# Graph network of four layers: masks of the edge sums made for four tiles by one instruction, records waited for by fours

## The chip, the cores and the metric

One core of one Trainium2 chip. The metric is the device time of one execution in microseconds; before the change it is 5067.49 us, the median of three runs (5064.09 to 5072.64). Differences of about 0.2%, 10 us, can be told from none.

## The reference

6250 nodes with 256 features (x), 100000 edges sorted by target (src, dst), with 128 attributes, a type (0 to 15) and a weight. Each of four layers adds to x what it makes of h = relu(layernorm(x)):

```python
# layer 0: weighted sums by source
out = segment_sum((h @ weight)[dst] * edge_weight[:, None], src) + b
# layer 1: sums of edge attributes by source, degrees, two gates
h + z_in[in_deg] + z_out[out_deg] + cent_term + vor_term + segment_sum(edge_attr @ W_sum + b_sum, src)
# layer 2: attention over the edges of a target, then a feed-forward part
# layer 3: sums by target of neighbour rows and relation vectors, then a GRU cell
red = segment_sum(h[src] + relvectors[edge_type], dst)
out = gru_cell(red, h, w_ih, w_hh, b_ih, b_hh)
```

Everything is float32. Layers 0 and 1 need sums by source, layer 3 sums by target.

## The kernel before

All stages work on edges that are sorted and cut into 832 tiles of 128 edges (TILES); the nodes stand in 49 blocks of 128 (BLOCKS), and each tile holds edges of one block. A sum over the edges of a tile is a product on TensorE (PE): a mask (hot) with a one in row e, column n where edge e belongs to node n of the block, times the rows of the 128 edges. VectorE (DVE) makes the mask by comparing the row of numbers 0 to 127 (iota) with the edge's local node, and adds the product from PSUM to the block's sums in SBUF.

The stages follow each other:

1. `prepare`: ranks the edges by source and scatters their records (attributes, source, weight, target) to `src_records`, 784 indirect DMAs by POOL (L462).
2. `sources_and_layers_0_1`: per tile SP loads 128 records (L932), POOL gathers 128 rows of h (`gather`, L983), DVE makes `hot` (`hots`, L1198) and `hotw`, hot times the weight (`weigh`, L1203), PE makes two products (`sum_rows`, L1018, L1019), DVE adds them (`add`, L1211). Between the tiles the steps of layers 0 and 1 for each finished block are woven in, one block each 16 tiles: among them two gathers of z by POOL (`gather_z`, L993) that wait for degrees from DVE, and two powers by POOL (`root`, L1003) that wait for variances from DVE (L1282).
3. `attention`: 832 tiles with gathers (L1398), masks and products of its own.
4. `layer_2`, dense work on blocks.
5. `relations_and_layer_3`: per tile POOL gathers 128 rows (L2005), DVE makes `hot` (L2178) and, in columns 256 to 271 of the gathered row, the mask of the edge's type (L2182), PE makes one product (L2046), DVE adds it (L2190). The steps of the GRU are woven in.

The helper `woven` writes out each engine's order by hand: at position n it calls each step of a tile with a lag, step(n - lag), and each step of a block at its own position. In stage 2 DVE runs at position n: add of tile n-4 (LAG), weigh of n-1, hots of n, then node steps; all node steps of DVE stand DVE_LEAD = 2 positions behind the listed ones, those of POOL POOL_LEAD = 5 behind. Each engine runs its queue in order and waits at semaphores. Rings: 16 slots for records and rows (R), 8 for masks (H), 4 PSUM banks for the sums. A slot's reuse waits for PE's count of finished tiles (`summed`), a bank's reuse for DVE's count of adds. POOL waits for each tile's record with `own_wait`, a wait and a nop.

## Time and profile before

| | us |
|---|---|
| median of three runs | 5067.49 |
| lowest, highest | 5064.09, 5072.64 |
| span of the profiled execution | 6606.6 |
| PE busy in it | 3748.5 |
| DVE busy | 3700.6 |
| POOL busy | 3595.2 |
| ACT busy | 1475.8 |

Only the span is told of the profiled execution; it is 1539.1 us longer than the median of the runs without recording. The stages' borders in it are read from POOL's and the other engines' first and last instructions: prepare up to 1499 us, sums by source 1499 to 3152, attention to 4911, layer 2 to 5226, relations to the end. The chain of waits covers only the last per cent of the span, so it isn't used.

### The profile page before, as it was taken

The numbers are of one execution on the slowest core, as the hardware profiler recorded it, in microseconds if no ns is written. First come the engines' busy times: TensorE is split into PE (matmuls) and PEld (weight loads), VectorE is DVE, ScalarE is ACT, GpSimd is POOL, SyncE is SP. The second block draws the span as 40 slices with busy tenths as digits, with TensorE's granted clock in tenths as the row PEclk, the third lists the DMA queues.
The fourth block names the chain that finished last, engine by engine and source line by source line (L and its number), as shares of the span: only waits on it lengthen the run. The fifth ranks groups of instructions, "written<-read, shape, count | busy, mean of one in ns | idle before, by whom it ended". The sixth has DMA issues, their size and how long they took to land. (4 is left out here: it accounts for less than half of the span.)

```text
span 6606.6 us, 98591 instructions
## 1 busy us (share of the span) xinstructions
PE 3748.5 (57%) x15612; PEld 2748.4 (42%) x15613; DVE 3700.6 (56%) x12722; ACT 1475.8 (22%) x5078; POOL 3595.2 (54%) x4000
## 2 busy tenths in 40 slices
PE   0000020005776776776677777777779667777676
PEld 0000010004555554555455555555559534444443
DVE  5249691006666666666555555555557656555555
ACT  1000000000111111111455455555546301100000
POOL 4640686755655565555444444444437766655554
PEclk9999999998887888888788888878889878888888
DMA  4320224454444444444333333333332233333332
GB/s 119 85 68 0 73 83 89 118 148 120 127 127 123 125 128 124 127 128 111 93 94 94 96 95 95 94 93 94 97 95 86 89 88 94 91 91 90 90 90 72
DMA packets 505174, 651.54 MB, mean 99 GB/s; under 512 B 86113, under 2 KB 381294, under 8 KB 504944
## 3 DMA queue, kind: packets, MB, share of 16 engines
q0 software_dynamic: 150160, 395.04, 20.9%
q1 hardware_dynamic: 354913, 255.45, 14.3%
q14 instruction: 73, 0.60, 0.0%
q8 instruction: 28, 0.46, 0.0%
HBM read 550.09 MB, written 100.06 MB: 98 GB/s over the span
## 5 line engine op out<-in xcount | busy, mean ns | idle before, releaser
L1398 POOL DMA_INDIRECT a_row<-h_rows,a_idx x832 | 789.8, 949 | 944.0 <-PE a_p_s L1504 396.0
L2005 POOL DMA_INDIRECT r_row<-h_rows,r_idx x832 | 798.3, 960 | 528.7 <-PE r_p_s L2046 267.9
L462 POOL DMA_INDIRECT src_records<-rec,pos_slot x784 | 808.2, 1031 | 419.6 <-issue 250.3
L983 POOL DMA_INDIRECT s_row<-h_rows,s_rec x832 | 804.5, 967 | 281.0 <-issue 242.2
L1018 PE MATMUL s_sums<-s_row,s_hotw 128*128 128x256 f32 x1664 | 661.3, 484 | 519.5 <-DVE s_hotw L1203 315.3
L2046 PE MATMUL r_p_s<-r_row,r_hot 128*128 128x272 f32 x1664 | 644.8, 502 | 362.8 <-DVE r_row L2182 171.9
L1481 PE MATMUL a_p_q<-nodes,a_hotT 128*128 x1664 | 665.0, 486 | 314.9 <-DVE a_score L1551 188.9
L1211 DVE TENSOR_TENSOR nodes<-nodes,s_sums 128x385 f32 x832 | 455.5, 548 | 509.1 <-remote 290.8
L1504 PE MATMUL a_p_s<-a_row,a_masked 128*128 128x257 f32 x1664 | 588.7, 439 | 178.1 <-issue 124.3
L2046 PEld LDWEIGHTS r_p_s<-r_row,r_hot 128*128 128x128 f32 x1664 | 353.1, 234 | 678.8 <-issue 296.2
L1551 DVE CUSTOM_DVE_ANT_0 a_prod<-a_p_q,a_row 128x258 f32<-128x258 f32 x832 | 352.7, 424 | 415.9 <-DMA s_rec<-src_records 187.6
L1018 PEld LDWEIGHTS s_sums<-s_row,s_hotw 128*128 128x128 f32 x1664 | 301.9, 223 | 677.5 <-DVE s_hotw L1203 373.2
L1588 DVE SCALAR_TENSOR_TENSOR sums<-sums,a_fade,a_p_s 128x257 f32 x832 | 399.9, 481 | 263.1 <-DMA s_row<-h_rows,s_rec 141.5
L2190 DVE TENSOR_TENSOR sums<-sums,r_p_s 128x272 f32 x832 | 358.1, 430 | 300.5 <-PE r_p_s L2046 137.5
L1504 PEld LDWEIGHTS a_p_s<-a_row,a_masked 128*128 128x128 f32 x1664 | 353.1, 221 | 287.1 <-issue 183.7
L576 PE MATMUL p_total<-cnt,ones 128*128 128x49 f32 x4 | 1.3, 432 | 813.9 <-issue 783.3
L1481 PEld LDWEIGHTS a_p_q<-nodes,a_hotT 128*128 128x128 f32 x1664 | 293.7, 221 | 334.7 <-issue 333.2
L1019 PEld LDWEIGHTS s_sums<-s_rec,s_hot 128*128 128x128 f32 x1664 | 374.8, 225 | 69.4
L1433 ACT ACTIVATE a_masked<-a_far,a_score 128x128 f32<-128x128 f32 x832 | 326.5, 392 | 224.7 <-issue 191.8
L1019 PE MATMUL s_sums<-s_rec,s_hot 128*128 128x129 f32 x1664 | 368.4, 308 | 0.0
L576 PEld LDWEIGHTS p_total<-cnt,ones 128*128 128x128 f32 x4 | 1.0, 312 | 813.7 <-issue 783.5
L1496 PEld LDWEIGHTS a_p_l<-a_m,a_hotT 128*128 128x128 f32 x1664 | 291.2, 219 | 84.1 <-issue 33.8
(315 smaller groups left out, 7511.6 us busy)
## 6 DMA issues: line engine op xcount, KB each, us to landing
s_rec<-src_records SPq DMA_DIRECT2D x832, 66.0 KB
a_locs<-dloc_rows SPq DMA_DIRECT2D x208, 256.0 KB
rec<-in_edge_attr SPq DMA_DIRECT2D x98, 448.0 KB
s_row<-h_rows,s_rec POOLq DMA_INDIRECT x832
a_row<-h_rows,a_idx POOLq DMA_INDIRECT x832
r_row<-h_rows,r_idx POOLq DMA_INDIRECT x832
src_records<-rec,pos_slot POOLq DMA_INDIRECT x784
x_rows<-X SPq DMA_DIRECT2D x1, 6272.0 KB
```

The source lines that it names most:

```text
L462: gp.indirect_dma_start(out=src_records, out_offset=bass.IndirectOffsetOnAxis(ap=pos_slot[:, k:k + 1], axis=0), in_=rec[:, k, :], in_offse ...
L983: gp.indirect_dma_start(out=row[:, k % R, :], out_offset=None, in_=env["h0_rows"], in_offset=bass.IndirectOffsetOnAxis(ap=rec[:, k % R, DS ...
L1018: nc.tensor.matmul(bank[:, 0:D], hotw[:, k % H, :], row[:, k % R, :], start=True, stop=True)
L1019: nc.tensor.matmul(bank[:, D:NW], hot[:, k % H, :], rec[:, k % R, 0:ED + 1], start=True, stop=True).then_inc(summed, 1)
L1211: nc.vector.tensor_tensor(s, s, sums[k % BANKS][:, 0:NW], ALU.add).then_inc(block_added, 1)
L1398: gp.indirect_dma_start(out=row[:, k, 0:D], out_offset=None, in_=env["h2_rows"], in_offset=bass.IndirectOffsetOnAxis(ap=idx[:, k:k + 1], a ...
L1481: nc.tensor.matmul(p_q[k % 2], hotT[:, k % F, :], query[:, bass.ds(b, 1), 0:RW].rearrange("p a d -> p (a d)"), start=True, stop=True).then ...
L1504: nc.tensor.matmul(p_s[k % 2], masked[:, k % F, :], row[:, k, 0:D + 1], start=True, stop=True).then_inc(S["summed"], 1)
L1588: nc.vector.scalar_tensor_tensor(out=s, in0=s, scalar=fade[:, k % F:k % F + 1], in1=p_s[k % 2], op0=ALU.mult, op1=ALU.add).then_inc(S["add ...
L2005: gp.indirect_dma_start(out=row[:, k % R, 0:D], out_offset=None, in_=env["h3_rows"], in_offset=bass.IndirectOffsetOnAxis(ap=idx[:, k:k + 1 ...
L2046: nc.tensor.matmul(p_s[k % 4], hot[:, k % H, :], row[:, k % R, :], start=True, stop=True).then_inc(S["summed"], 1)
L2190: nc.vector.tensor_tensor(s, s, p_s[k % 4], ALU.add).then_inc(S["added"], 1)
```

## The change

In stage 2 the rings of masks grow to 16 slots. At every fourth tile DVE does for four tiles at once: `locate` (new; source minus the block's base, 4 columns), `hots` (iota equal to that column) and `weigh` (mask times weight), each one `tensor_tensor` with broadcast operands where there was one `tensor_scalar` per tile. The adds are done 8 tiles behind, and DVE's node steps stand 4 positions later. The four records of a group signal one semaphore; POOL waits once in four tiles, PE for the weighted masks too. In stage 5 the two masks are made for four tiles by one instruction each, the type masks first; the mask ring stays at 8 slots.

```diff
+FOUR = 4
@@ sources_and_layers_0_1
-    R, H = SLOT, UNROLL
-    LAG = 4
+    R, H = SLOT, SLOT
+    BLOCKS_READ = UNROLL
+    LAG = 8
-    SP_LEAD, POOL_LEAD, DVE_LEAD = 16, 5, 2
+    SP_LEAD, POOL_LEAD, DVE_LEAD = 16, 5, 6
+        local = sb(ctx, "s_local", [P, H])
-        rec_in = [sem(f"s_rec_in{k}") for k in range(R)]
+        rec_in = [sem(f"s_rec_in{k}") for k in range(R // FOUR)]
+        def four_of(k, g):
+            return g * (WOVEN // FOUR) + k // FOUR
+        def slot_in(eng, k, g):
+            eng.wait_ge(rec_in[k % R // FOUR], turn_of(k, g) * (16 * FOUR) + 16 * FOUR)
...
                 def gather(i, k, opening, g):
-                    own_wait(gp, rec_in[k % R], turn_of(k, g) * 16 + 16)
+                    if k % FOUR == 0:
+                        slot_in(gp, k, g)
+                        gp.nop(nofuse=True)
...
                 def sum_rows(i, k, opening, g):
-                    pe.wait_ge(hotw_ready, i + 1)
+                    if k % FOUR == 0:
+                        pe.wait_ge(hotw_ready, four_of(k, g) + 1)
...
+                def locate(i, k, opening, g):
+                    if k % FOUR:
+                        return
+                    slot_in(ve, k, g)
+                    if not opening or k >= H:
+                        ve.wait_ge(hot_ready, four_of(k, g) - (H // FOUR - 1))
+                    nc.vector.tensor_tensor(local[:, slots(k)].rearrange("p (k o) -> p k o", o=1), rec[:, slots(k), SRC:SRC + 1],
+                                            pbase[:, bass.ds(i, FOUR)].rearrange("p (k o) -> p k o", o=1), ALU.subtract
+                                            ).then_inc(local_ready, 1)
                 def hots(i, k, opening, g):
-                    ve.wait_ge(rec_in[k % R], turn_of(k, g) * 16 + 16)
+                    if k % FOUR:
+                        return
+                    ve.wait_ge(local_ready, four_of(k, g) + 1)
                     if not opening or k >= H:
-                        ve.wait_ge(summed, i - H + 1)
-                    nc.vector.tensor_scalar(hot[:, k % H, :], c["iota"][:], pbase[:, bass.ds(i, 1)], rec[:, k % R, SRC:SRC + 1],
-                                            ALU.add, ALU.is_equal).then_inc(hot_ready, 1)
+                        ve.wait_ge(summed, i - (H - FOUR))
+                    nc.vector.tensor_tensor(hot[:, slots(k), :], c["iota"].rearrange("p (a n) -> p a n", a=1).broadcast_to([P, FOUR, P]),
+                                            column(local[:, slots(k)].rearrange("p (k o) -> p k o", o=1)), ALU.is_equal
+                                            ).then_inc(hot_ready, 1)
                 def weigh(i, k, opening, g):
-                    ve.wait_ge(hot_ready, i + 1)
-                    nc.vector.tensor_scalar(hotw[:, k % H, :], hot[:, k % H, :], rec[:, k % R, WGT:WGT + 1], None,
+                    if k % FOUR:
+                        return
+                    ve.wait_ge(hot_ready, four_of(k, g) + 1)
+                    nc.vector.tensor_tensor(hotw[:, slots(k), :], hot[:, slots(k), :], column(rec[:, slots(k), WGT:WGT + 1]),
                                             ALU.mult).then_inc(hotw_ready, 1)
...
-                woven(ve, (LAG, add), (1, weigh), (0, hots), once={24: [key_bias]}, begin=load_blocks,
+                woven(ve, (LAG, add), (2, weigh), (1, hots), (0, locate), once={24: [key_bias]}, begin=load_blocks,
@@ relations_and_layer_3
                 def sum_rows(i, k, opening, g):
-                    pe.wait_ge(S["hot_ready"], i * 2 + 2)
+                    if k % FOUR == 0:
+                        pe.wait_ge(S["hot_ready"], (g * (WOVEN // FOUR) + k // FOUR) * 2 + 2)
...
                 def hots(i, k, opening, g):
+                    if k % FOUR:
+                        return
+                    if not opening or k >= R:
+                        ve.wait_ge(S["summed"], i - (R - FOUR))
+                    nc.vector.tensor_tensor(row[:, k % R:k % R + FOUR, D:DW], row_of(RELS), column(c["dtyp"], i, RELS),
+                                            ALU.is_equal).then_inc(S["hot_ready"], 1)
                     if not opening or k >= H:
-                        ve.wait_ge(S["summed"], i - H + 1)
-                    nc.vector.tensor_scalar(hot[:, k % H, :], c["iota"][:], c["dloc"][:, bass.ds(i, 1)], None,
-                                            ALU.is_equal).then_inc(S["hot_ready"], 1)
-                    if not opening or k >= R:
-                        ve.wait_ge(S["summed"], i - R + 1)
-                    nc.vector.tensor_scalar(row[:, k % R, D:DW], c["iota"][:, 0:RELS], c["dtyp"][:, bass.ds(i, 1)], None,
+                        ve.wait_ge(S["summed"], i - (H - FOUR))
+                    nc.vector.tensor_tensor(hot[:, k % H:k % H + FOUR, :], row_of(P), column(c["dloc"], i, P),
                                             ALU.is_equal).then_inc(S["hot_ready"], 1)
```

## Rows read from the trace of the kernel before

**Rows 1.** The page, part 1: busy us (share of the span), instructions.
```profile
PE 3748.5 (57%) x15612; PEld 2748.4 (42%) x15613; DVE 3700.6 (56%) x12722; ACT 1475.8 (22%) x5078; POOL 3595.2 (54%) x4000
```

**Rows 2.** Groups by line, POOL: busy us, mean ns | idle before, releasers.
```profile
L462 POOL DMA_INDIRECT src_records<-rec,pos_slot x784 | 808.2, 1031 | 419.6 <-issue 250.3 <-ACTq L542 157.8 <-remote 11.4
L983 POOL DMA_INDIRECT s_row<-h_rows,s_rec x832 | 804.5, 967 | 281.0 <-issue 242.2 <-DMA s_rec<-src_records 33.1 <-DVE n_vare L1282 5.5
L2005 POOL DMA_INDIRECT r_row<-h_rows,r_idx x832 | 798.3, 960 | 528.7 <-PE r_p_s L2046 267.9 <-issue 216.4 <-DMA pair<-in_dst 41.7
L1398 POOL DMA_INDIRECT a_row<-h_rows,a_idx x832 | 789.8, 949 | 944.0 <-PE a_p_s L1504 396.0 <-ACT a_idx L1413 337.3 <-issue 210.6
...
L1003 POOL TENSOR_TENSOR n_rstd<-n_vare,n_half 128x1 f32<-128x1 f32 x98 | 55.3, 565 | 231.0 <-DVE n_vare L1282 218.6 <-issue 12.4
...
L993 POOL DMA_INDIRECT z<-in_L_gnn_z_in,deg x49 | 47.7, 974 | 166.2 <-DVE deg L1225 161.4 <-issue 4.9
L993 POOL DMA_INDIRECT z<-in_L_gnn_z_out,deg x49 | 47.3, 965 | 14.9 <-issue 14.9
```

**Rows 3.** Timeline, sums by source: start, us, engine, what [idle before <-releaser].
```profile
2508.78 0.95 POOL L983 DMA_INDIRECT s_row<-h_rows,s_rec  x1 [0.30 <-issue]
...
2510.03 0.95 POOL L983 DMA_INDIRECT s_row<-h_rows,s_rec  x1 [0.30 <-issue]
2512.74 0.56 DVE L1211 TENSOR_TENSOR nodes<-nodes,s_sums 128x385 f32 x1 [4.21 <-remote]
2512.85 0.49 ACT L1139 ACTIVATE turned<-p_t 128x384 f32<-128x384 f32 x1 [3.68 <-remote]
```

**Rows 4.** Timeline of POOL: in the preparation, and its last instruction.
```profile
677.63 8.23 POOL L473 TENSOR_TENSOR rstd<-vare,half 128x49 f32<-128x49 f32 x1 [220.98 <-DVE vare L175]
...
6551.61 0.95 POOL L2005 DMA_INDIRECT r_row<-h_rows,r_idx  x1 [0.38 <-issue]
```

**Rows 5.** Windows, source and relations: us, busy PE PEld DVE ACT POOL, PEclk, DMA, GB/s.
```profile
1499.00:3152.00 1653.00, 1146.81 (x4279) 845.76 (x4279) 1038.43 (x3430) 173.97 (x400) 954.88 (x1028) 0.82 0.45 124
...
5226.00:6607.00 1381.00, 995.69 (x2923) 583.33 (x2923) 776.26 (x2841) 133.03 (x458) 798.32 (x832) 0.82 0.31 90
```

**Rows 6.** Groups by line, DVE: a tensor_tensor of 256, a reduction over 512.
```profile
L1561 DVE TENSOR_REDUCE a_tmax<-a_p_m 128x4 f32<-128x512 f32 x208 | 142.4, 685 | 45.6 <-PE a_p_m L1488 33.2 <-issue 7.9 <-DMA s_rec<-src_records 4.4
...
L1250 DVE TENSOR_TENSOR added_terms<-added_terms,sig 128x256 f32<-128x256 f32 x98 | 40.7, 415 | 0.0
```

**Rows 7.** Timeline of DVE where nothing holds it: source, then relations.
```profile
2503.39 0.54 DVE L1211 TENSOR_TENSOR nodes<-nodes,s_sums 128x385 f32 x1
2503.86 0.27 DVE L1203 TENSOR_SCALAR s_hotw<-s_hot,s_rec 128x128 f32<-128x128 f32 x1
2504.05 0.33 DVE L1198 TENSOR_SCALAR s_hot<-iota,s_pbase,s_rec 128x128 f32<-128x128 f32 x1
2504.31 0.54 DVE L1211 TENSOR_TENSOR nodes<-nodes,s_sums 128x385 f32 x1
...
5605.71 0.43 DVE L2190 TENSOR_TENSOR sums<-sums,r_p_s 128x272 f32 x1
5606.06 0.28 DVE L2178 TENSOR_SCALAR r_hot<-iota,dloc 128x128 f32<-128x128 f32 x1
5606.40 0.43 DVE L2190 TENSOR_TENSOR sums<-sums,r_p_s 128x272 f32 x1
```

**Rows 8.** Timeline, source: a node step on DVE beside a gather.
```profile
2500.89 0.42 DVE L1250 TENSOR_TENSOR added_terms<-added_terms,sig 128x256 f32<-128x256 f32 x1
2501.00 1.16 POOL L983 DMA_INDIRECT s_row<-h_rows,s_rec  x1 [0.19 <-issue]
```

**Rows 9.** Timeline, preparation: masks for eight steps on DVE beside scatters.
```profile
898.70 1.31 POOL L462 DMA_INDIRECT src_records<-rec,pos_slot  x1 [0.30 <-issue]
899.56 1.21 DVE L782 TENSOR_TENSOR oh_lo<-iota_b,lo_d 128x1024 bf16<-128x1024 bf16 x1
...
900.32 1.31 POOL L462 DMA_INDIRECT src_records<-rec,pos_slot  x1 [0.31 <-ACTq L542]
```

More of the change, by code:

```diff
@@ L874, in sources_and_layers_0_1 @@
         tables, based, cleared = sem("s_tables"), sem("s_based"), sem("s_cleared")
[L875 removed]
+        rec_in = [sem(f"s_rec_in{k}") for k in range(R // FOUR)]
         row_in = [sem(f"s_row_in{k}") for k in range(R)]
[L877 removed]
+        local_ready, hot_ready, hotw_ready = sem("s_local_ready"), sem("s_hot_ready"), sem("s_hotw_ready")
         summed, block_added = sem("s_summed"), sem("s_added")
@@ L931, in load_records @@
                         sp.wait_ge(summed, i - R + 1)
-                    sp.dma_start(rec[:, k % R, :], env["src_records"][bass.ds(firsts[k % 4], P), :]).then_inc(rec_in[k % R], 16)
+                    sp.dma_start(rec[:, k % R, :], env["src_records"][bass.ds(firsts[k % 4], P), :]).then_inc(rec_in[k % R // FOUR], 16)
                 def load_weights():
@@ L1188, in load_blocks, with slots @@
                 def load_blocks(i, k):
-                    if k % H == 0:
+                    if k % BLOCKS_READ == 0:
                         _, blocks[:] = nc.values_load_multi_w_load_instructions(
-                            blk[0:1, bass.ds(i + (PAD - LAG), H)], engines=(DVE_E,), min_val=0, max_val=BLOCKS - 1,
+                            blk[0:1, bass.ds(i + (PAD - LAG), BLOCKS_READ)], engines=(DVE_E,), min_val=0, max_val=BLOCKS - 1,
                             skip_runtime_bounds_check_because=BLOCK_RANGE)
+                def slots(k):
+                    return slice(k % R, k % R + FOUR)
@@ new lines, in column @@
+                def column(t):
+                    return t.broadcast_to([P, FOUR, P])
+                def locate(i, k, opening, g):
[7 more added lines that the diff above has]
+                                            ).then_inc(local_ready, 1)
@@ L1204, in weigh @@
+                    ve.wait_ge(hot_ready, four_of(k, g) + 1)
+                    nc.vector.tensor_tensor(hotw[:, slots(k), :], hot[:, slots(k), :], column(rec[:, slots(k), WGT:WGT + 1]),
                                             ALU.mult).then_inc(hotw_ready, 1)
                 def add(i, k, opening, g):
-                    b = blocks[(k + LAG) % H]
+                    b = blocks[(k + LAG) % BLOCKS_READ]
                     ve.wait_ge(summed, i + 1)
@@ L2173, in load_blocks, with column, row_of @@
                             skip_runtime_bounds_check_because=BLOCK_RANGE)
+                def column(t, i, w):
+                    return t[:, bass.ds(i, FOUR)].rearrange("p (k o) -> p k o", o=1).broadcast_to([P, FOUR, w])
+                def row_of(w):
+                    return c["iota"][:, 0:w].rearrange("p (a n) -> p a n", a=1).broadcast_to([P, FOUR, w])
                 def hots(i, k, opening, g):
-                    if not opening or k >= H:
-                        ve.wait_ge(S["summed"], i - H + 1)
-                    nc.vector.tensor_scalar(hot[:, k % H, :], c["iota"][:], c["dloc"][:, bass.ds(i, 1)], None,
-                                            ALU.is_equal).then_inc(S["hot_ready"], 1)
-                    if not opening or k >= R:
-                        ve.wait_ge(S["summed"], i - R + 1)
-                    nc.vector.tensor_scalar(row[:, k % R, D:DW], c["iota"][:, 0:RELS], c["dtyp"][:, bass.ds(i, 1)], None,
+                    if k % FOUR:
[4 more added lines that the diff above has]
+                                            ALU.is_equal).then_inc(S["hot_ready"], 1)
+                    if not opening or k >= H:
+                        ve.wait_ge(S["summed"], i - (H - FOUR))
+                    nc.vector.tensor_tensor(hot[:, k % H:k % H + FOUR, :], row_of(P), column(c["dloc"], i, P),
                                             ALU.is_equal).then_inc(S["hot_ready"], 1)
```

1 line of the change is left out of this document (removed).

## Prediction

> **What bounds the kernel now.** I read the engines' busy times first, then the groups by line, then one stretch of the timeline. The recorded execution spans 6606.6 us, the median of the runs is 5067.5 us: recording adds 1539 us, 30%. The sums below are made of durations of the recorded execution, so I must first say which of its time is also in the unrecorded runs.
>
> POOL is busy 3595.2 us [rows 1]. Nearly all of it is indirect DMAs: 784 scatters, 3 x 832 row gathers, 98 gathers of z, 3378 in all [rows 2]. Back to back they follow each other with 0.30 us of idle between them (2508.78, 2510.03: 1.25 us apart, 0.95 us busy) [rows 3]. 3378 x 0.30 = 1013 us, so POOL's queue alone needs 3595 + 1013 = 4608 us. Outside the loops it waits 221.0 us for the ranking, and 54 us remain after its last gather [rows 4]. That makes 4883 of the 5067.5 us. All its other waits together may be at most 184 us in an unrecorded run; in the recorded one they are 6606.6 - 4883 = 1724 us. What they are is seen in [rows 3]: VectorE and ScalarE both stand still for some 4 us with nothing named that holds them, while POOL goes on. I take these halts for a thing of the recording. So unrecorded the gathers set the pace.
>
> By stage: the sums by source (1653 us recorded) hold 804.5 + 95.0 + 55.3 us of POOL and 930 gaps, 1234 us; the relations (1381 us) 798.3 + 832 x 0.30 = 1048 us [rows 2]. VectorE is busy 1038 and 776 us there, PE 1147 and 996 us at a mean granted clock of 0.82, between its two levels [rows 5]. PE is thus next, at 93% and 95% of POOL's time, and VectorE, which the change relieves, third.
>
> **The change part by part.** *Masks by source.* Per four tiles eight tensor_scalar (four hots, four weighs) become one small subtraction (locate) and two tensor_tensor over 512 elements. No row has a tensor_tensor of 512 float32; the 256 wide one takes 415 ns, a reduction over 512 takes 685 ns [rows 6], 1.05 ns an element. I take 0.68 us for a mask of four, 0.21 us for the type mask (64 elements); locate lies between nothing and that, I take 0.21. *On VectorE:* undisturbed, it passes a tile each 0.92 us, 0.47 of it for the add; in the relations each 0.69 us, 0.35 for the add [rows 7]. Operations overlap by 0.07 us there, so a mask costs 0.61 and a small one 0.14. Source, per four: 3.68 before, 4 x 0.47 + 2 x 0.61 + 0.14 = 3.24 after; x 208 groups = -92 us. Relations: 2.76 before, 4 x 0.35 + 0.61 + 0.14 = 2.15 after; -127 us. VectorE gains 219 us, beside POOL's gathers: nothing of it is on the path.
>
> *On POOL the masks cost something.* At 2500.89 a 0.42 us tensor_tensor with two SBUF inputs is running when a gather starts at 2501.00. The gather takes 1.16 instead of 0.95 us: 0.21 longer, as much as the operation lasts beyond 0.10 us after the gather's start [rows 8]. The next gather follows 0.30 us after that end, so the delay is in POOL's pace. The same form as the new masks, iota broadcast against a column per tile, stands in the preparation: 1.21 us each, and the scatters beside it take 1.31 us and come each 1.62 us [rows 9]; there POOL runs at VectorE's pace. The adds (L1211, with a PSUM input) run beside gathers of 0.95 us and cost nothing, and the old masks cost little: gathers average 967 and 960 ns where these masks run, 949 in the attention, 18 and 11 ns, together at most 24 us, part of which belongs to L1250 [rows 2].
>
> So each new mask is a lock of 0.68 us that a gather's read may fall into. With no phase preferred, a gather period of 1.26 us is hit with a chance of 0.68/1.26 = 0.54 and then waits 0.34 us, 0.18 us. The second mask comes one tile after the first; a gather already pushed behind the first mostly escapes it, so I count half, 0.09. Source: 0.27 x 208 = 56 us, all of it on the path. Relations: type mask and mask stand together, 0.14 + 0.68 = 0.82 us; 0.66 x 0.41 = 0.27, x 208 = 56 us, of which I count half, since POOL waits there 267.9 us for free slots from PE [rows 2], and a late gather falls partly into such a wait. The old masks' disturbance goes: -10 us, within 0 and -24. Bounds: no hit at all 0; every mask hit at its start 2 x 0.68 x 208 = 283 us and 0.82 x 208 = 171 us.
>
> The Trainium skill (SBUF — State Buffer, Who interferes with whom) states that a VectorE instruction with two SBUF inputs contends with a GpSimd instruction that reads SBUF, and the second to issue blocks fully. The same section infers that descriptor generation needs the write interface only, and that tensor_tensor does not stall it: by that the cost would be nothing, as in the second rival below. What this case shows [rows 8, 9] speaks for the first sentence.
>
> *Waits of POOL.* Three of four waits with their nops go. They are passed early while POOL works on earlier gathers: the gap is 0.30 us in the source loop and in the preparation alike [rows 3, 9]. Gain: nothing; 0.01 us each, the grain of these rows, would be 8 us. The wait that is left asks for four records; behind it stand the gathers, the gathers of z and the roots. It lets POOL be 13 tiles ahead of PE, not 16; 13 x 1.25 = 16 us of cover. At the start three more records are awaited once, under 5 us.
>
> *Order.* The adds lie 8 behind, not 4, and VectorE's node steps 4 later (DVE_LEAD 6), so counted in PE's tiles they wait for the same sums. POOL_LEAD stays 5: gather_z and root now stand 2 positions behind their VectorE step, not 6. As VectorE may now be 8 tiles ahead of PE, this costs nothing while masks are ready; if that cover is gone, each of 49 nodes could pay 4 positions less of slack, which is what POOL's waits of 161.4 and 218.6 us for VectorE already show in the recorded run [rows 2]. In the relations the mask ring stays at 8: masks for tiles i to i+3 stand behind the add of tile i-4, and PE then has three tiles left, 3.8 us of gathers, against 0.35 + 0.75 us of VectorE. Hidden. PE's work is unchanged.
>
> **The sum.** 5067.5 + 56 + 28 - 10 = 5142 us.
>
> **The rivals.** *First, faster: VectorE's relief arrives.* The halts of [rows 3] would then be partly in the unrecorded runs too, and POOL's waits for VectorE (380 us in the source stage, [rows 2]) would be real ones. For it: they are most of the 419 us by which that stage exceeds POOL's need. Against it: all waits left are 184 us. It decides where VectorE, not a row's arrival, ends PE's or POOL's wait last. Price: half of the 184 us, 4975 us; all of it, 4883. In a sentence of its own: the Trainium skill (VectorE: DVE Perf Modes, Rules for kernel authors) says to minimize the count of operations, which is this rival's rule.
>
> *Second, nothing moves.* The masks' place against the gathers is fixed by the chain gather, sum, add; if the read falls beside both masks, nothing is lost, and VectorE was not the bound: 5067 within 10 us. For it: VectorE waits for sums that POOL paces, so the phase may be steady.
>
> *Third, slower by the new order.* POOL, 2 positions behind, waits for VectorE in each node step, some 1.3 us each for 3 steps of 49 nodes, 190 us: 5258 us. It decides if VectorE lags PE by more than its 8 tiles.
>
> **How the numbers follow.** The forecast (delayed gathers) 0.47, own range 5080 to 5270; first rival 0.32; second 0.16; third 0.05. Faster by over 0.2% (10 us, about what a measurement can tell) 0.32; the same 0.15; slower 0.53. The range must reach both signs: 4960 to 5270 leaves out the deep end of the first rival and masks that are always hit.
>
> **What would show it.** In the profile after: the masks x208 at 0.65 to 0.75 us; the mean of the gathers L983 and L2005 up from 967 and 960 ns to some 1010 to 1050, the attention's 949 unchanged; 1.25 us spacing elsewhere; VectorE's instructions down by 2288 from 12722. Whatever the recorded span does says little on the time, as halts fill it. I am wrong if the gathers' means stay, or if they grow and the time falls: then VectorE or PE, not POOL, set the pace of these stages.

## The result

The changed kernel takes 5099.64 us, the median of four runs (5095.23 to 5105.28); the kernel before, measured beside it, 5069.80 (5064.09 to 5072.64). The ratio is 1.0062, with a 95% interval of 1.0048 to 1.0076: slower by some 31 us (the medians lie 30 apart). The forecast was 5142.

The record of before that stands ahead of the prediction was disturbed by halts of the recording. A second record of the same kernel (`e0_before_again`) spans 5060.7 us, a run's own time, and has no halts; it is the one that is compared from here on. The record of after spans 5093.4 us. In after the lines have moved: the gathers are L994, L1431 and L2038 (before L983, L1398, L2005), in the source stage `hots` is L1228, `weigh` L1236, `locate` L1218, the add L1244, in the relations the type mask is L2220, the mask L2224, the add L2232, PE's product L2080.

The first row below is part 1 of after's page and answers [rows 1]; the others are after's groups of POOL, answering [rows 2] (busy us, mean ns | idle before, releasers).

```profile
PE 3243.2 (64%) x15612; PEld 2481.0 (49%) x15613; DVE 3444.5 (68%) x10434; ACT 1454.8 (29%) x5078; POOL 3644.2 (72%) x4000
...
L994 POOL DMA_INDIRECT s_row<-h_rows,s_rec x832 | 830.7, 998 | 253.1 <-issue 238.7 <-DMA s_rec<-src_records 13.8 <-DVE n_vare L1315 0.6
L2038 POOL DMA_INDIRECT r_row<-h_rows,r_idx x832 | 814.4, 979 | 322.7 <-issue 165.3 <-PE r_p_s L2080 145.0 <-ACT r_idx L2140 12.4
...
L1431 POOL DMA_INDIRECT a_row<-h_rows,a_idx x832 | 792.7, 953 | 282.6 <-issue 181.8 <-PE a_p_s L1537 68.6 <-ACT a_idx L1446 32.1
...
L1014 POOL TENSOR_TENSOR n_rstd<-n_vare,n_half 128x1 f32<-128x1 f32 x98 | 58.9, 601 | 15.6 <-DVE n_vare L1315 13.7
```

The same groups in the undisturbed record of before:

```profile
L983 POOL DMA_INDIRECT s_row<-h_rows,s_rec x832 | 812.5, 977 | 249.6 <-issue 231.8 <-DMA s_rec<-src_records 16.6 <-DVE n_vare L1282 0.6
...
L2005 POOL DMA_INDIRECT r_row<-h_rows,r_idx x832 | 805.8, 968 | 319.0 <-PE r_p_s L2046 160.1 <-issue 157.7 <-ACT r_idx L2106 1.2
L1398 POOL DMA_INDIRECT a_row<-h_rows,a_idx x832 | 790.0, 950 | 283.2 <-issue 182.4 <-PE a_p_s L1504 64.1 <-ACT a_idx L1413 36.7
...
L1003 POOL TENSOR_TENSOR n_rstd<-n_vare,n_half 128x1 f32<-128x1 f32 x98 | 59.2, 605 | 17.9 <-DVE n_vare L1282 16.1
```

In the relations POOL has nothing but gathers, so their row gives the stage's length almost by itself, busy plus idle: before 805.8 + 319.0 = 1124.8 us and after 814.4 + 322.7 = 1137.1. In the source stage the gathers got 18.2 us longer, the idle ahead of them 3.5. In the attention, whose gathers had no part in the change, busy grew by 2.7. From the start of a stage's first gather to the end of its last:

| stage, us | before (second record) | after | |
|---|---|---|---|
| sums by source | 1237.8 | 1256.2 | +18.4 |
| attention | 1069.0 | 1071.4 | +2.4 |
| relations | 1123.8 | 1136.3 | +12.5 |

That is 33.3 us, and the spans differ by 32.7: the two changed stages lost 30.9, the attention 2.4, and nothing else lost. The relief of VectorE is there too, 3644.9 us busy before and 3444.5 after, with no gain in time. PE's clock is not the reason, since the granted clock rose, in source from 0.91 to 0.95 and in the relations from 0.85 to 0.89.

The new operations on VectorE, in after's source stage and then in its relations:

```profile
L1228 DVE TENSOR_TENSOR s_hot<-iota,s_local 128x512 f32<-128x512 f32 x208 | 142.5, 685 | 0.1
L1236 DVE TENSOR_TENSOR s_hotw<-s_hot,s_rec 128x512 f32<-128x512 f32 x208 | 142.3, 684 | 0.1
...
L1218 DVE TENSOR_TENSOR s_local<-s_rec,s_pbase 128x4 f32<-128x4 f32 x208 | 32.8, 158 | 1.0 <-DMA s_rec<-src_records 1.0
...
L2224 DVE TENSOR_TENSOR r_hot<-iota,dloc 128x512 f32<-128x512 f32 x207 | 142.9, 690 | 0.0
L2220 DVE TENSOR_TENSOR r_row<-iota,dtyp 128x64 f32<-128x64 f32 x207 | 45.3, 219 | 0.8 <-DVE sums L2199 0.7
```

And one collision, on after's timeline (start us, us, what):

```profile
1370.97 0.54 DVE L1244 TENSOR_TENSOR nodes<-nodes,s_sums 128x385 f32 x1
...
1371.43 0.68 DVE L1236 TENSOR_TENSOR s_hotw<-s_hot,s_rec 128x512 f32<-128x512 f32 x1
1371.44 1.49 POOL L994 DMA_INDIRECT s_row<-h_rows,s_rec  x1 [0.30 <-issue]
```

The weighted mask ends at 1372.11. The gather, 0.95 us long by itself, lasts until 1372.93: 0.82 us beyond the mask's end, as if it had done 0.13 of its 0.95 us when the mask held it up. In 73 of the 208 weighted masks and 37 of the 208 masks a gather was at that point while the mask ran, and took 0.253 and 0.257 us longer on average: 28 us in all. In the relations 85 of 208 masks did so, by 0.253 us: 21.5 us.

The distance of 0.82 us tells which operation made a gather late. Nearly every gather over 0.03 us longer than the median of its stage ends 0.74 to 0.87 us after the end of a VectorE operation. By this sign the late gathers of before, 18.5 us in source and 18.9 in the relations, are mostly not the single masks' doing (6.5 and 1.3 us). The rest, 11.7 and 17.4 us, goes to node steps with two SBUF inputs, like this one of the GRU in the second record of before:

```profile
4234.88 0.42 DVE L2216 TENSOR_TENSOR nodes<-g_step,nodes 128x256 f32 x1
4234.94 1.18 POOL L2005 DMA_INDIRECT r_row<-h_rows,r_idx  x1 [0.30 <-issue]
```

After, the masks of four make 28.1 and 21.6 us late, the node steps 8.2 and 5.9. So the change brought its own locks and, by a shifted phase, took some of the node steps' away.

### The profile page after: what moved, and what is told of

Same layout as the page of the kernel before. It is cut to its first block and busy times, and to the rows that moved or that the text cites. A ratio compares the mean times of both kernels' runs of the same rounds, so it can differ in the third digit from the quotient of the medians.

```text
span 5093.4 us, 93142 instructions
## 1 busy us (share of the span) xinstructions
PE 3243.2 (64%) x15612; PEld 2481.0 (49%) x15613; DVE 3444.5 (68%) x10434; ACT 1454.8 (29%) x5078; POOL 3644.2 (72%) x4000
## 3 DMA queue, kind: packets, MB, share of 16 engines
q1 hardware_dynamic: 354913, 255.45, 18.4%
## 5 line engine op out<-in xcount | busy, mean ns | idle before, releaser
L2038 POOL DMA_INDIRECT r_row<-h_rows,r_idx x832 | 814.4, 979 | 322.7 <-issue 165.3
L994 POOL DMA_INDIRECT s_row<-h_rows,s_rec x832 | 830.7, 998 | 253.1 <-issue 238.7
L1431 POOL DMA_INDIRECT a_row<-h_rows,a_idx x832 | 792.7, 953 | 282.6 <-issue 181.8
L1030 PE MATMUL s_sums<-s_row,s_hotw 128*128 128x256 f32 x1664 | 590.0, 439 | 381.4 <-DMA s_row<-h_rows,s_rec 230.7
L2080 PE MATMUL r_p_s<-r_row,r_hot 128*128 128x272 f32 x1664 | 591.4, 470 | 270.1 <-DVE r_hot L2224 258.0
L1514 PE MATMUL a_p_q<-nodes,a_hotT 128*128 x1664 | 570.3, 425 | 77.8 <-issue 77.1
L2080 PEld LDWEIGHTS r_p_s<-r_row,r_hot 128*128 128x128 f32 x1664 | 341.1, 222 | 532.3 <-DVE sums L2232 284.0
L1244 DVE TENSOR_TENSOR nodes<-nodes,s_sums 128x385 f32 x832 | 460.0, 553 | 154.8 <-PE s_sums L1031 116.5
L2232 DVE TENSOR_TENSOR sums<-sums,r_p_s 128x272 f32 x832 | 363.0, 436 | 263.6 <-PE r_p_s L2080 147.4
L1537 PE MATMUL a_p_s<-a_row,a_masked 128*128 128x257 f32 x1664 | 497.8, 381 | 1.0 <-ACT a_masked L1487 0.5
L1031 PEld LDWEIGHTS s_sums<-s_rec,s_hot 128*128 128x128 f32 x1664 | 342.3, 206 | 54.0
L1031 PE MATMUL s_sums<-s_rec,s_hot 128*128 128x129 f32 x1664 | 341.8, 289 | 0.0
L1537 PEld LDWEIGHTS a_p_s<-a_row,a_masked 128*128 128x128 f32 x1664 | 313.0, 190 | 50.6 <-issue 3.3
L1458 ACT ACTIVATE a_far<-iota,dloc 128x128 f32<-128x128 f32 x832 | 323.4, 389 | 0.0
L1487 ACT ACTIVATE a_masked<-a_masked,a_mneg 128x128 f32<-128x128 f32 x832 | 323.3, 389 | 0.0
```

The lines of the kernel that those rows point to most:

```text
L994: gp.indirect_dma_start(out=row[:, k % R, :], out_offset=None, in_=env["h0_rows"], in_offset=bass.IndirectOffsetOnAxis(ap=rec[:, k % R, DS ...
L1030: nc.tensor.matmul(bank[:, 0:D], hotw[:, k % H, :], row[:, k % R, :], start=True, stop=True)
L1031: nc.tensor.matmul(bank[:, D:NW], hot[:, k % H, :], rec[:, k % R, 0:ED + 1], start=True, stop=True).then_inc(summed, 1)
L1244: nc.vector.tensor_tensor(s, s, sums[k % BANKS][:, 0:NW], ALU.add).then_inc(block_added, 1)
L1431: gp.indirect_dma_start(out=row[:, k, 0:D], out_offset=None, in_=env["h2_rows"], in_offset=bass.IndirectOffsetOnAxis(ap=idx[:, k:k + 1], a ...
L1514: nc.tensor.matmul(p_q[k % 2], hotT[:, k % F, :], query[:, bass.ds(b, 1), 0:RW].rearrange("p a d -> p (a d)"), start=True, stop=True).then ...
```

## The experiments

Two theories for the two stages. **Locks**: a VectorE operation with two SBUF inputs that runs when a gather reads SBUF delays the gather until it ends. **Lateness**: in the relations the group's masks come out later than the single ones did, because a step ahead of them in VectorE's queue waits. Against both, the rivals: the new order or its waits cost the time, or the loss is spread over what the record doesn't show. The runs follow in three groups; "relations" and the other stage lengths are measured as in the table above.

### Which stage, and an undisturbed record

`e0_before_again` is the kernel before, unchanged.

> The kernel before, unchanged, recorded again, since its first record spans 6606.6 us against runs of 5070 us while the record of the changed kernel spans 5093.4 us. Recording theory (the 4 us halts of VectorE and ScalarE belong to that one record): span within 1% of 5070 us, no idle of VectorE ended by an unknown queue, gathers of the source stage at 950 to 960 ns on average, of the relations at 946 to 955 ns. Relief theory (the halts come with the many small instructions of this kernel): the halts are there again and the span is above 5500 us.

5062.73 us, span 5060.7. No halt as in [rows 3] is left, so they were the recording's. `e1_source_only` has the change in stage 2 alone, `e2_relations_only` in stage 5 alone; in each the other stage is that of before.

```diff
 # e1: relations as before
-                    nc.vector.tensor_tensor(hot[:, k % H:k % H + FOUR, :], row_of(P), column(c["dloc"], i, P),
+                    nc.vector.tensor_scalar(hot[:, k % H, :], c["iota"][:], c["dloc"][:, bass.ds(i, 1)], None,
...
 # e2: sums by source as before
-    R, H = SLOT, SLOT
-    LAG = 8
+    R, H = SLOT, UNROLL
+    LAG = 4
...
```

> Only the source stage is changed; the relations stay as before. The record of the changed kernel holds 110 gathers of the source stage whose read fell into a mask and that were 0.25 us late each, 28 us, and 85 in the relations, 21 us. Delayed-gather theory: +15 to +30 us over before. Order theory (the groups of four and the longer lag hold POOL or PE up): the difference lies in the relations, where the mask ring has only 8 slots, so within 8 us of before here. Relief theory: faster than before by 10 us or more here, and the loss is all in the relations.

> Only the relations are changed. Delayed-gather theory: 85 late gathers, 21 us, of which half is absorbed by waits for PE: +5 to +20 us. Order theory: PE waits 258 us for the mask of four in the record of the changed kernel, so +20 us or more, close to the whole +31 us. Relief theory: 0 or below.

| | median us | ratio to before (95%) | source | relations |
|---|---|---|---|---|
| e1_source_only | 5083.68 | 1.0033 (1.0021 to 1.0045) | 1255.9 | 1123.1 |
| e2_relations_only | 5085.92 | 1.0042 (1.0028 to 1.0056) | 1239.8 | 1141.3 |

Each part costs some 0.3 to 0.4%. Their sum, 0.75%, agrees with the whole's 0.62% within the intervals. In e1 the source gathers take 999 ns and the relations' 970; in e2 979 and 980. Source's loss is all in the gathers' length, as the locks have it. Kernels that leave the source stage as it was take 1236.8 to 1239.8 us there, so its 18 us stand clear. The relations' loss is not all in the gathers: of the 17.5 us of e2, 9.4 are in their length (805.8 to 815.2 us busy) and 8.0 in POOL's idle time (319.0 to 327.0). That is a sum, not a split by cause, as two kernels with before's relations unchanged show (`e6` and `e10`, below):

```profile
L2014 POOL DMA_INDIRECT r_row<-h_rows,r_idx x832 | 798.4, 960 | 327.0 <-issue 180.2 <-PE r_p_s L2055 144.5 <-ACT r_idx L2115 2.4
```

```profile
L2014 POOL DMA_INDIRECT r_row<-h_rows,r_idx x832 | 809.3, 973 | 313.7 <-issue 161.9 <-PE r_p_s L2055 150.3 <-ACT r_idx L2115 1.5
```

The gathers differ by 10.9 us, and the stage takes 1124.5 and 1122.1 us all the same: in this order the waits take up what the gathers lose. How much of e2's 17.5 us is locks and how much lateness, these rows can't tell.

### Is it the two inputs?

`e6_spare_two_inputs` and `e7_spare_one_input` are the kernel before with one spare operation in each group of four tiles of the source stage. It reads an array of zeros and writes one that nobody reads. In e6 it is the new mask's form, with two SBUF inputs; in e7 a reduction of the same 512 elements, with one.

```diff
+                    if k % 4 == 0:
+                        if not opening or k >= 4:
+                            ve.wait_ge(spared, g * (WOVEN // 4) + k // 4)
 # e6
+                        nc.vector.tensor_tensor(spare_out[:], c["iota"].rearrange("p (a n) -> p a n", a=1).broadcast_to([P, 4, P]),
+                                                spare_in[:], ALU.is_equal).then_inc(spared, 1)
 # e7
+                        nc.vector.tensor_reduce(spare_out[:, :, 0], spare_in[:], AX.X, ALU.max).then_inc(spared, 1)
```

> The kernel before, with one spare instruction more on VectorE once in four tiles of the source stage, behind weigh: a tensor_tensor of 4 x 128 with two SBUF inputs, whose result nobody reads, about 0.69 us. Delayed-gather theory: +10 to +40 us, source gathers' mean up by 10 to 45 ns. Relief theory (VectorE's time counts): the same as the next kernel, +50 us and more in both.

> The same place and about the same length (0.68 us), but a tensor_reduce of 4 x 128, one SBUF input. Delayed-gather theory: within 6 us of before, gathers' mean unchanged (977 ns in the record of before). Relief theory: as much as the two-input one.

e6 takes 5227.91 us (ratio 1.0320, 1.0305 to 1.0334), e7 5192.39 (1.0251, 1.0237 to 1.0265). Most of both is a stall in the attention that has nothing to do with the question (1203.6 and 1199.0 us there; see below). In the source stage, where the operation stands, the two differ as the locks ask: 1271.6 us in e6, 1236.1 in e7, 1237.8 before. The operations are as long, 684 and 679 ns, and as many. One meeting of each, e6 first, then e7:

```profile
1701.17 0.68 DVE L1212 TENSOR_TENSOR s_spare_out<-iota,s_spare_in 128x512 f32<-128x512 f32 x1
1701.39 1.30 POOL L986 DMA_INDIRECT s_row<-h_rows,s_rec  x1 [0.30 <-issue]
```

```profile
1572.05 0.68 DVE L1212 TENSOR_REDUCE s_spare_out<-s_spare_in 128x4 f32<-128x512 f32 x1
1572.07 0.95 POOL L986 DMA_INDIRECT s_row<-h_rows,s_rec  x1 [0.30 <-issue]
```

In e7 the gather starts 0.02 us into the operation and isn't delayed. So it was on average for the 78 gathers of e7 that met one (0.00 us), while 97 of e6 took 0.22 us longer, 21.7 us in all. The stage grew by more than that, since the spare operation also moved a node step with two SBUF inputs (L1264) onto 47 gathers, 18.0 us; before, the same step had delayed 7, by 0.9 us. Both are locks. The two spare operations differ in one thing more: the reduction writes 4 elements, the mask 512. The adds (L1244), which write 385 and read one input from PSUM, delay nothing either, so it is not the writing. That settles the locks: it is not VectorE's time that costs, but the second SBUF input.

`e10_spare_two_inputs_moved` is e6 with more empty instructions ahead of attention's loop.

```diff
-                for _ in range(38):
+                for _ in range(38 + 199):
```

> The kernel of e6_spare_two_inputs (the kernel before, with one spare two-input instruction of VectorE per group of four tiles in the source stage, whose result nobody reads), with 199 more empty instructions ahead of attention's loop. Placement theory: attention falls from 1203.6 to about 1069 us, source stays at 1270 to 1272 us with its gathers at about 1010 ns, and the whole takes 5095 to 5105 us, so that the spare instructions cost what their locks on the gathers cost, 30 to 40 us, in the kernel's time too. Rival: attention stays at 1204 and the kernel at 5228.

5114.90 us (ratio 1.0096, 1.0080 to 1.0111), source 1274.1 us, attention 1088.9. 115 us of the stall are gone, and the locks' 36 us of the source stage are in the kernel's time. The attention keeps 20 us over its 1069.0, which the runs don't explain; hence 5115 and not the 5095 to 5105 expected.

### What makes the relations late

`e3_groups_of_scalar` keeps the groups and the order of the change, but makes each mask by an instruction of its own with one SBUF input; `e9_groups_of_scalar_moved` is e3 with 71 empty instructions more ahead of attention's loop. The edit for one of the four masks, the others likewise:

```diff
-                    nc.vector.tensor_tensor(hot[:, k % H:k % H + FOUR, :], row_of(P), column(c["dloc"], i, P),
-                                            ALU.is_equal).then_inc(S["hot_ready"], 1)
+                    for j in range(FOUR):
+                        last = nc.vector.tensor_scalar(hot[:, k % H + j, :], c["iota"][:], c["dloc"][:, bass.ds(i + j, 1)], None,
+                                                       ALU.is_equal)
+                    last.then_inc(S["hot_ready"], 1)
```

> The changed kernel with all its groups, lags, rings and waits, but each mask made by four tensor_scalar of 128 elements (type masks of 16) in a row, with one signal after the fourth, in both stages; locate stays. It keeps the order and takes the long two-input instructions away. Delayed-gather theory: back to before, 5060 to 5080 us, and gathers of both stages under 965 ns on average. Order theory: stays at 5095 us or above, as the masks of a group come even later (four times 0.2 us and more). Relief theory: above the changed kernel by the VectorE time given back.

> The kernel of e3_groups_of_scalar (the groups of the change, each mask made by a single instruction with one SBUF input), with 71 more empty instructions on VectorE just ahead of attention's loop, so that the loop lies at the same place of VectorE's program as in the kernel before. Placement theory: VectorE's stall of up to 5 us once per iteration of attention's loop goes, attention falls from 1195.7 to about 1070 us, and the kernel takes 5165 to 5180 us. Rival, that the stall comes from the order of the work or from buffers that come free late: attention stays near 1196 and the kernel at 5298. Both expect relations to stay near 1229 us (a group of four single masks of 0.41 us or more comes right after VectorE's wait, and TensorE waits for it), since nothing there is changed.

e3: 5298.18 us (ratio 1.0460, 1.0446 to 1.0475); source 1232.9 with gathers of 971 ns, attention 1195.7, relations 1229.1 with gathers of 957. e9: 5169.86 us (1.0210, 1.0194 to 1.0225); attention 1077.1, relations 1222.2. Two things at once. Without the second input the locks go, in both stages, as expected. But the relations lost 105 us all the same, with shorter gathers: groups of four single masks in a row cost more than the locks did. PE waited 323.5 us for r_hot in e3, 198.9 for the type mask, the later of the two, in before.

The timeline of e2 shows what the groups stand behind:

```profile
4438.79 0.44 DVE L2200 TENSOR_TENSOR sums<-sums,r_p_s 128x272 f32 x1 [0.88 <-PE r_p_s L2048]
...
4442.79 1.03 PE L2089 MATMUL g_p_n<-g_w_hh,g_turned 128*128 128x256 f32 x4
...
4443.65 0.62 PE L2048 MATMUL r_p_s<-r_row,r_hot 128*128 128x272 f32 x2
4443.85 0.42 DVE L2210 TENSOR_TENSOR g_cand<-g_p_n,g_b_hn 128x256 f32<-128x256 f32 x1 [4.63 <-PE g_p_n L2089]
...
4445.77 0.44 DVE L2200 TENSOR_TENSOR sums<-sums,r_p_s 128x272 f32 x1 [0.58 <-issue]
4446.12 0.22 DVE L2188 TENSOR_TENSOR r_row<-iota,dtyp 128x64 f32<-128x64 f32 x1
4446.26 0.68 DVE L2192 TENSOR_TENSOR r_hot<-iota,dloc 128x512 f32<-128x512 f32 x1
...
4447.16 1.27 PE L2048 MATMUL r_p_s<-r_row,r_hot 128*128 128x272 f32 x2 [2.89 <-DVE r_hot L2192]
```

VectorE's first candidate step of the GRU (L2210) waits 4.63 us for PE's last product of that block. Meanwhile PE works through the tiles whose masks are ready, the last at 4443.65, and then stands still for 2.89 us: its next mask is behind the candidate's three steps, an add and the type mask. This comes once a block. VectorE waits 231.9 us there in e2's relations, and 215.1 in before's, where it was the same place with shorter masks behind.

Two ways out, each with single masks as of before. One makes masks and adds earlier against PE: `e8_scalar_masks_lag8` has 16 masks and adds eight behind, the GRU's steps moved by four so that they stay where they were against the adds. `e11_scalar_masks_lag8_gru6` moves them two more. `e5_relations_lag8` is e2 (groups, two inputs) with the order of e8.

```diff
-    R, H = SLOT, UNROLL
-    LAG = 4
+    R, H = SLOT, SLOT
+    LAG = 8
...
-                woven(ve, (LAG, add), (0, hots), nodes=[(STATE, state), (CAND, candidate_in)], once={6: [biases]},
+                woven(ve, (LAG, add), (0, hots), nodes=[(STATE + 4, state), (CAND + 4, candidate_in)], once={6: [biases]},
```

> Source stage as before. Relations with the masks of four, but the mask ring has 16 slots, the adds lie 8 tiles behind instead of 4, and VectorE's GRU steps stand 4 positions later: the masks of a group are then ready while VectorE waits for PE's candidate sums. Late-mask theory (PE waits 254 us for the mask of four, 59 us more than for the single masks before, since a group's 0.85 us comes just after that wait, once a block): relations 12 to 40 us shorter than in the run with the relations alone changed (1141 us of gathers), so 5045 to 5075 us, and PE's wait for the mask under 100 us. Delayed-gather theory alone: no change against the relations alone, 5080 to 5090 us, since the two-input instructions stay.

> The kernel before with single masks by tensor_scalar in both stages, and in the relations alone the ring of 16, the adds 8 behind and the GRU steps 4 positions later. Late-mask theory: PE's 195 us of waits for r_row shrink, 10 to 25 us faster than before, 5040 to 5055 us. If the banks (adds), not the masks, hold PE after VectorE's wait: within 5 us of before.

> The kernel of e8_scalar_masks_lag8 with the steps of the recurrent update two positions later still (+6 in place of +4). If TensorE's wait for VectorE's adds (176 us in relations of e8) is caused by adds that stand behind VectorE's own wait for the candidate sums, that wait shrinks and relations fall from 1082 to 1060 to 1075 us, the kernel to 5000 to 5012. If GpSimd's gathers (704 of them at about 1.25 us each, 880 us, and the scatters) or TensorE's own chain set it by now, relations stay at 1080 and the kernel at 5018 to 5022. If the later update now holds up the state's way back at the end of a block, it grows to 5030.

| | median us | ratio (95%) | relations | POOL: busy + idle | PE's largest wait |
|---|---|---|---|---|---|
| e5 | 5089.55 | 1.0053 (1.0039 to 1.0067) | 1145.9 | 831.9 + 314.9 | adds 167.2 |
| e8 | 5019.92 | 0.9912 (0.9897 to 0.9927) | 1082.2 | 798.7 + 284.4 | adds 178.8 |
| e11 | 4977.77 | 0.9830 (0.9816 to 0.9843) | 1049.9 | 796.7 + 254.0 | adds 79.7 |

With masks ahead PE no longer waits for them but for the adds, which free its PSUM banks and stand behind the same candidate step; two positions more take that away. e8 and e11 gained more than expected. e5 did not do what lateness asked of it, 12 to 40 us less than e2 in the relations: it took 4.6 us more. Between e8 and e5 only the masks' form and their grouping differ, and they cost 64 us there: 33 in the gathers' length, 31 in POOL's waits. Why the waits grew stays open. PE's waits for VectorE are no longer in e5 (211.6 us against 221.6), but its products are busy for 943 us at a granted clock of 0.86, against 875 at 0.94, and no run tells whether that is the cause or follows from the stage's length.

The other way moves only the GRU's steps by two positions and keeps the read-ahead: `e12_relations_gru2` on e2, `e13_before_gru2` on the kernel before, `e14_after_gru2` on the changed kernel, `e15_groups_of_scalar_gru2` on e9.

```diff
-                woven(ve, (LAG, add), (0, hots), nodes=[(STATE, state), (CAND, candidate_in)], once={6: [biases]},
+                woven(ve, (LAG, add), (0, hots), nodes=[(STATE + 2, state), (CAND + 2, candidate_in)], once={6: [biases]},
```

> The kernel of e2_relations_only (the change in relations alone, groups of four and the read-ahead of four kept), with the candidate and state steps of the recurrent update two positions later. Late-mask theory: VectorE waits less before the group's mask, TensorE's wait for r_hot falls well under 253 us, and the kernel takes 5055 to 5080 us against 5085.9 for e2; the extension of the gathers stays near 29 us. Contention alone: only the gathers' extension counts, it is unchanged, and the time stays at 5084 to 5088.

> The kernel before with the candidate and state steps of the recurrent update in relations two positions later, as in e12, and nothing of the change. If the late mask was most of the 17.5 us that the groups cost in relations, the single masks were late too (TensorE waited 195 us for them) and gain less from the move: relations 1060 to 1068 us here against 1067.9 in e12, so that the groups cost 0 to 8 us there. If the locks on the gathers are what the groups cost, relations are 9 to 16 us shorter here than in e12 (28.2 us of extension there against 12 to 19 here): 1052 to 1059 us, and the kernel 4975 to 4982. If the move helps only the groups, relations stay near 1124 and the kernel at 5063.

> The whole change with the same move of two positions. The stages add up: source 1256, relations 1067 to 1070, in all 5005 to 5015 us, against e13 by 20 to 35 us more, most of it the source stage's 18. A rival by which the stages interact (other placement of a loop, other phase) gives more than 5020 or less than 5000.

> The kernel of e9 (groups of four one-input masks, attention's loop back at its old place) with the same move. Late-mask theory: the group's 1.7 us no longer stand behind VectorE's wait, relations fall from 1222 to 1050 to 1100 us and the kernel from 5170 to 5000 to 5050. If four masks in a row hold up the adds, and TensorE through its banks, by themselves, relations stay above 1180 and the kernel above 5130.

| | median us | ratio (95%) | source | relations |
|---|---|---|---|---|
| e12 (groups in relations) | 4991.11 | 0.9856 (0.9841 to 0.9871) | 1238.6 | 1067.9 |
| e13 (kernel before) | 4980.65 | 0.9820 (0.9805 to 0.9835) | 1237.8 | 1049.6 |
| e14 (changed kernel) | 5016.20 | 0.9896 (0.9880 to 0.9911) | 1254.8 | 1069.8 |
| e15 (groups, one input) | 4984.89 | 0.9831 (0.9813 to 0.9849) | 1233.2 | 1053.7 |

A block in e12: the candidate step waits 1.60 us where it waited 4.63, and PE then stands 0.47 us, for an add, where it stood 2.89 for a mask.

```profile
4440.32 0.44 DVE L2200 TENSOR_TENSOR sums<-sums,r_p_s 128x272 f32 x1
...
4442.16 1.54 PE L2048 MATMUL r_p_s<-r_row,r_hot 128*128 128x272 f32 x6
4442.36 0.42 DVE L2210 TENSOR_TENSOR g_cand<-g_p_n,g_b_hn 128x256 f32<-128x256 f32 x1 [1.60 <-PE g_p_n L2089]
...
4444.16 0.72 PE L2048 MATMUL r_p_s<-r_row,r_hot 128*128 128x272 f32 x2 [0.47 <-DVE sums L2200]
```

The gathers' groups in relations, of e12's and then of e13's POOL:

```profile
L2006 POOL DMA_INDIRECT r_row<-h_rows,r_idx x832 | 814.7, 979 | 254.0 <-issue 153.2 <-PE r_p_s L2048 99.3 <-ACT r_idx L2108 1.5
```

```profile
L2005 POOL DMA_INDIRECT r_row<-h_rows,r_idx x832 | 796.2, 957 | 254.2 <-issue 176.2 <-PE r_p_s L2046 75.6 <-ACT r_idx L2106 2.4
```

The move gained far more than the 6 to 31 us expected of e12: 73.4 us of the relations with groups (e2 to e12) and 74.2 with single masks (before to e13). So the waits that it ends were nearly all in the kernel before already, and not brought by the change. PE went faster with it, a granted clock of 0.85 in before's relations and of 0.98 in e13's; what of the 74 us came by way of the clock isn't separated.

Idle is 254 us in both, and in e11 and e15: 0.305 us per gather. That is the 0.30 us between gathers that follow back to back, whoever the row names for it, so POOL now waits for nobody in this stage. There the stage is 832 x (gather + 0.305 us), and whatever lengthens a gather is in the time whole. e12 less e13: 814.7 - 796.2 = 18.5 us by the rows, 18.3 by the stages, 0.36% (18 us) by the ratios, each of which has 0.15% of doubt; the medians as they stand differ by 10.5 us, but the kernel before, run beside each, was some 8 us slower beside e13. My expectation for e13 had asked for late masks or locks; it was the second, and a bit more than the 9 to 16 us it named. For the groups with one input the move took 168.5 us out of the relations (e9's 1222.2 to e15's 1053.7, against 1049.6 in e13): their loss was lateness, all but 4 us. e14 costs 35.6 us more than e13, 17.0 in source and 20.2 in relations: 37.2 by the stages, nearly all of it locks (its gathers are busy 39.1 us longer). 5016 is 1 us over the 5005 to 5015 expected.

The change's groups thus cost the relations as much with the move (18.3 us) as without it (17.5). With it, it is locks. Without it, a late mask and a late gather can hide one behind the other, and their shares are not shown.

e13 is also the version that beats both kernels, by changing two numbers; e11 and e15 are equal to it within their intervals.

## Why the direction was right and the size wrong

The direction held, and its cause in the source stage. The size failed, 74 us of net cost against 31: the locks were worked out at 56 + 28 us, and the two stages lost 18.4 and 12.5. In the relations the prediction also missed that masks come late there.

**What bounds the kernel.** That the halts were a thing of the recording is confirmed by the second record. That POOL sets the pace held for the source stage: its gathers' idle before is 249.6 us for 832, 0.30 each, and the stage grew by just what the gathers did. In the relations it did not hold. POOL's idle before is 319.0 us, 65 more than its own pace needs. The prediction had left 184 us for waits and did not ask where they are; 65 of them are here, and moving the GRU's two steps brought the time to 0.98 (e13).

**Costs on VectorE.** Masks: 0.68 us foreseen, 0.685 to 0.690 measured. Type mask 0.21, measured 0.219. `locate` 0.21, measured 0.158. The gain of 219 us was to be worth nothing. VectorE is busy 200 us less, and the kernel is slower: held.

**Locks.** The mechanism read from two meetings [rows 8, 9] is right: the delay runs to the end of the operation, adds with a PSUM input delay nothing (276 gathers of after met one of L1244 and were on average no longer for it), and e6 against e7 shows that the second SBUF input makes it. Here the Trainium skill (SBUF — State Buffer, Who interferes with whom) was weighed: its inference that tensor_tensor does not stall the making of descriptors is not what these runs show. Its sentence on VectorE instructions with two SBUF inputs agrees with them.

**Their size** is the term that failed. In source the sum had 0.54 + 0.27 hits a group, 168 hits of 0.34 us, 56 us. The trace has 110 hits (73 of 208 weighted masks, 37 of 208 masks) of 0.25 us, 28 us: hits are fewer than with no phase preferred, as the second rival half argued, and fall later in the mask. Why the phase is as it is I haven't shown. The places are the other way round, too: the first mask of a group was counted in full (112 hits) and had 37, the second was counted by half (56) and had 73. So the gathers came out at 998 and 979 ns, 977 and 968 in the undisturbed record of before, and not at the 1010 to 1050 named. The relief of 10 us is near the 9.7 that lie between the 28.1 us of the new locks and the 18.4 measured, but not for the reason given: 6.5 us of it are the single masks', 3.5 node steps that now meet fewer gathers. In relations 56 us were worked out and 21.5 measured (85 hits of 0.253 us).

**Counting half of it** for the relations, since POOL waits there anyway, was a guess at cover. Half of the 21.5 us of locks would be 11, and 12.5 to 17.5 were measured, which is near by luck: the gathers grew by 8.6 us only because the GRU's steps, with two SBUF inputs of their own, hit them for 11.5 us less than before, and what lateness adds isn't separated. With the cover gone the locks cost 18 (e12 against e13).

**"Hidden" was wrong.** The prediction let the relations' masks stand behind the add of tile i-4 and gave PE three tiles, 3.8 us. Between that add and the mask stands, once a block, the candidate step with a wait of its own of 4.63 us; the cover was spent. [rows 7] shows VectorE only where nothing holds it, and the steps of the GRU have no row at all: the queue had to be read at the position where it is worst. e9 against e15 prices it for the longer group of single masks, 168 us of the relations. For the change's own groups no run separates it from the locks; the two together are 17.5 us (e2).

**Waits of POOL and the order** in the source stage were put at nothing: POOL's waits for variances ahead of L1003 are 16.1 us before and 13.7 after. Held, and the third rival (190 us) with it fell.

**The first rival**, that VectorE's relief arrives, fell too. Its premise was half true: real waits were left, and they were worth 1.8% of the time (e13). But they were waits for the place of the GRU's steps in VectorE's queue, not for its load: a VectorE with 200 us less work gave nothing, the same work in another order 1.8%.

## What to carry to other kernels

Where an engine that isn't the bound gets fewer and longer instructions, look first at what those instructions lock and what stands behind them, not at the time they save: here 2288 instructions and 200 us less of VectorE cost 31 us. Prefer a form with one SBUF input beside a queue of gathers. And read each in-order queue at its worst place, behind the step with the longest wait of its own: moving it, with the step that follows it, by two positions gained 1.8%, three times what the whole change cost.

## What the runs showed that I had not expected

**A loop's place in the program.** e3, e6 and e7 change nothing in the attention, and each lost 127 to 135 us there. e3's timeline, POOL and VectorE at one such place (the same once in nearly every turn of the loop, 24 times, 4.2 to 5.2 us each), then the group of that operation in e3 and in e9:

```profile
2567.60 0.48 DVE L1624 SCALAR_TENSOR_TENSOR sums<-sums,a_fade,a_p_s 128x257 f32 x1
...
2569.99 0.95 POOL L1434 DMA_INDIRECT a_row<-h_rows,a_idx  x1 [0.30 <-issue]
...
2572.65 0.43 DVE L1587 CUSTOM_DVE_ANT_0 a_prod<-a_p_q,a_row 128x258 f32<-128x258 f32 x1 [4.57 <-issue]
```

```profile
L1587 DVE CUSTOM_DVE_ANT_0 a_prod<-a_p_q,a_row 128x258 f32<-128x258 f32 x832 | 350.3, 421 | 200.8 <-issue 115.3 <-PE a_p_q L1517 41.6 <-ACT a_masked L1469 40.1
```

```profile
L1587 DVE CUSTOM_DVE_ANT_0 a_prod<-a_p_q,a_row 128x258 f32<-128x258 f32 x832 | 350.4, 421 | 81.6 <-ACT a_masked L1469 69.7 <-PE a_p_q L1517 4.1 <-issue 3.5
```

VectorE stands for 4.57 us with nothing that the profile shows to wait for, at the back edge of its loop. 71 empty instructions ahead of the loop take that away (115.3 to 3.5 us of such idle, 1195.7 to 1077.1 us of attention; the 8 us left over 1069 are unexplained). Counted from where the loop stands in the kernel before, it is at -359 instructions in after and e1, at 0 in e8, e9 and e11, without the stall; at -71 in e3 and +57 in e6 and e7, with it; at +256 in e10, without the large one. The Trainium skill (Runtime: NRT & Kernel Launch, Instruction fetch mechanics) says that instructions are fetched in blocks of 256, and that a taken branch to a target outside the window of two blocks must wait for a fetch. A stall at the loop's back edge that goes by place is of that kind, but no run here shows that it is the fetch, and one limit per 256 instructions does not give these places: counted from before's place modulo 256 they are 0 and 153 without the stall, 57 and 185 with it, by turns, and e10, at 256, kept 20 us that 0 doesn't have. In the source stage of e6 and e7 VectorE has 58.1 and 53.2 us of such idle too, without a loss in e7's time there. An edit that adds or removes instructions ahead of a loop cost up to 2.7% here (135 us) in a stage that it didn't touch, so a comparison is to be read stage by stage.
